# Splitting the activation quantization around four matmul blocks, with four PSUM banks, in an attention and FFN kernel on eight cores

## The reference, cut to what matters

```python
def act_quant(x):
    scale = 127.0 / jnp.clip(jnp.max(jnp.abs(x), axis=-1, keepdims=True), 1e-05)
    return jnp.clip(jnp.round(x * scale), -128, 127) / scale
...
h = bit_linear(x, w1)                       # 1024 -> 4096, ternary weights
h = depthwise_conv1d(h.transpose(0, 2, 1), conv_w, conv_b)   # 3 taps along the sequence
h = h.transpose(0, 2, 1)
h = jax.nn.silu(h)
return bit_linear(h, w2)                    # quantizes h per token, 4096 -> 1024
```

## Time and profile before

| | |
|---|---|
| Time, median of 2 executions | 5146.94 us (5120.43 and 5173.45) |
| Profiled execution | 5137.58 us |
| Span of its slowest core, core 3 | 5135.8 us |
| Spans of the eight cores | 5099.2 to 5135.8 us |
| DVE busy | 3280.5 us (64%) |
| PE matmul busy | 1809.6 us (35%) |
| ACT busy | 967.7 us (19%) |

### The profile page before, as it was taken

One profiled execution on the slowest core, in us unless ns is written; L12 is line 12 of the kernel. 1 busy time (PEld: TensorE's weight loads), 2 busy tenths in 40 slices (PEclk: granted clock), 3 DMA queues, 4 the chain that ended last, 5 costly groups with the idle time before them and its releaser, 6 DMA issues. The chain is left out here.

```text
span 5135.8 us, 35109 instructions; the slowest of 8 cores (5099.2 to 5135.8 us)
## 1 busy us (share of the span) xinstructions
PE 1809.6 (35%) x8500; PEld 904.4 (18%) x8500; DVE 3280.5 (64%) x4522; ACT 967.7 (19%) x1773; POOL 25.7 (0%) x52
## 2 busy tenths in 40 slices
PE   0046433227433203222222222222223322205999
PEld 0022111013111102111111111111111111102444
DVE  3213577712377767777787777777778777774343
ACT  2200122200022202222232222322223222200111
POOL 0000000000000000000000000000000000000000
PEclk9987666657766656666666666666666666657999
DMA  5521111131211122000000000000000000025443
GB/s 166 142 31 47 60 41 41 41 51 17 82 43 41 45 104 63 1 22 22 22 23 0 22 22 23 22 0 22 22 22 22 1 22 17 17 90 174 142 160 107
DMA packets 189264, 258.95 MB, mean 50 GB/s; under 512 B 63490, under 2 KB 131330, under 8 KB 187012
## 3 DMA queue, kind: packets, MB, share of 16 engines
q1 hardware_dynamic: 163716, 197.95, 12.6%
q10 hardware_dynamic: 18432, 41.97, 2.1%
q0 software_dynamic: 6912, 16.78, 2.1%
HBM read 188.47 MB, written 75.52 MB: 51 GB/s over the span
## 5 line engine op out<-in xcount | busy, mean ns | idle before, releaser
L849 PE MATMUL ps_a<-xqF,tw 128*128 128x258 bf16 (+1 forms) x2048 | 364.8, 337 | 1386.7 <-DVE ubuf L860 1174.9
L587 PE MATMUL ps_s<-kf,qf 128*128 128x512 bf16 x1024 | 296.8, 461 | 605.6 <-ACT disc L604 603.2
L849 PEld LDWEIGHTS ps_a<-xqF,tw 128*128 128x128 bf16 x2048 | 222.9, 116 | 1523.1 <-issue 1462.4
L873 ACT ACTIVATE vt<-ubuf,cbcol,cwcol 128x256 f32<-128x256 f32 x512 | 307.8, 601 | 969.6 <-DVE ubuf L860 966.9
L849 PE MATMUL ps_b<-xqF,tw 128*128 128x258 bf16 (+1 forms) x2048 | 340.4, 320 | 107.5 <-DVE ubuf L860 106.4
L797 DVE TENSOR_TENSOR accb<-accb,rbuf 128x2048 bf16<-128x2048 bf16 x256 | 313.5, 1225 | 19.4 <-issue 0.4
L743 DVE SCALAR_TENSOR_TENSOR vt<-ubuf,cwcol,vt 128x256 f32<-128x256 f32 x512 | 248.2, 485 | 82.5 <-issue 65.6
L758 ACT ACTIVATE ubuf<-vt 128x256 f32<-128x256 f32 x512 | 213.8, 418 | 337.5 <-DVE vt L750 337.5
L750 DVE SCALAR_TENSOR_TENSOR vt<-ubuf,cwcol,vt 128x256 f32<-128x256 f32 x512 | 248.2, 485 | 39.7 <-issue 1.7
L1011 PE MATMUL ps_c<-tw,hq 128*128 128x512 bf16 x512 | 195.3, 381 | 202.2 <-DMA hq<-hqs 202.2
L849 PEld LDWEIGHTS ps_b<-xqF,tw 128*128 128x128 bf16 x2048 | 216.8, 113 | 224.7 <-issue 170.4
(11 more groups left out here) (134 smaller groups left out, 2795.8 us busy)
## 6 DMA issues: line engine op xcount, KB each, us to landing
hqs<-hqst SPq DMA_DIRECT2D x16, 2048.0 KB, 8.8
wstage<-w1T SPq DMA_DIRECT2D x8, 2048.0 KB, 8.7
wstage<-w2T SPq DMA_DIRECT2D x32, 512.0 KB, 4.4
xres<-x_tm SPq DMA_DIRECT2D x32, 512.0 KB, 3.3
x1s<-x1t ACTq DMA_DIRECT2D x32, 512.0 KB, 9.1
qstage<-w1T SPq DMA_DIRECT2D x8, 2048.0 KB, 8.2
qstage<-w2T SPq DMA_DIRECT2D x32, 512.0 KB, 3.5
xres<-x1s SPq DMA_DIRECT2D x32, 512.0 KB, 8.0
```

Of the source, the lines that this page charges most:

```text
L587: t.matmul(ps_s[kb][:, 0:KBW], qf[:, dc * S + qcol: dc * S + qcol + 128], kf[:, dc * S + kb * KBW: dc * S + (kb + 1) * KBW], start=(dc == ...
L849: lo=lo, hi=hi, w0=w0, W=W: t.matmul(bank[:, 0:W], tw[:, dc * H + hc * 128: dc * H + hc * 128 + 128], xqF[:, (par * DC + dc) * WW + (lo - w0):
L873: p.op("scalar", lambda sc, hc=hc: sc.activation(out=vt1[:, (hc % 4) * T1W2:(hc % 4) * T1W2 + T1], in_=ubuf[:, hc * T1W2 + 1:hc * T1W2 + 1 ...
```

## The change

The quantization of a group is cut in two functions. `emit_quant_A` (L771, L782) stays in front of blocks 0, 8, 16 and 24. `emit_quant_B` (the wait for ACT, L787 to L800) comes in front of blocks 4, 12, 20 and 28; the wait for the store of the tile before the quantized one goes with it. For the last tile A and B follow each other directly, as before. PE uses four banks in turn (ps_a, ps_b, ps_s[0], ps_s[1]) and waits for the L860 of four blocks earlier. The convolution's tails come three blocks behind instead of two. No operation is added, removed or changed in size.

```diff
-        def emit_quant_group(i, g0):
+        qg_iqq = {}
+
+        def emit_quant_A(i, g0):
             ng = min(NQG, HC - g0)
             FD = ng * T1
             s28 = s2bc8[:, 0:FD]
-            if g0 == 0:
-                if i >= 1:
-                    p.wait("vector", stsems[(i - 1) % 2], st_cnt[i - 1])
...
             p.op("scalar", lambda sc, FD=FD: sc.activation(
                 out=iqq[:, 0:FD], in_=zscr[:, 0:FD], func=AF.Identity,
                 bias=c128[:, 0:1], scale=1.0), inc=ssm)
-            ev_iqq = ssm.n
-            p.wait("vector", ssm, ev_iqq)
+            qg_iqq[(i, g0 // NQG)] = ssm.n
+
+        def emit_quant_B(i, g0):
+            ng = min(NQG, HC - g0)
+            FD = ng * T1
+            if g0 == 0:
+                if i >= 1:
+                    p.wait("vector", stsems[(i - 1) % 2], st_cnt[i - 1])
+            p.wait("vector", ssm, qg_iqq[(i, g0 // NQG)])
...
             for hc in range(HC):
-                bank = ps_a if hc % 2 == 0 else ps_b
+                bank = (ps_a, ps_b, ps_s[0], ps_s[1])[hc % 4]
                 cpar = hc % 2
                 if i >= 1 and hc % NQG == 0:
-                    emit_quant_group(i - 1, hc)
-                    if hc == 0:
-                        pass
-                if hc >= 2:
-                    p.wait("tensor", vv, ev_u[(i, hc - 2)])
+                    emit_quant_A(i - 1, hc)
+                if i >= 1 and hc % NQG == NQG // 2:
+                    emit_quant_B(i - 1, hc - NQG // 2)
+                if hc >= 4:
+                    p.wait("tensor", vv, ev_u[(i, hc - 4)])
                 elif i >= 1:
-                    p.wait("tensor", vv, ev_u[(i - 1, HC - 2 + hc)])
+                    p.wait("tensor", vv, ev_u[(i - 1, HC - 4 + hc)])
...
-                if hc >= 2:
-                    emit_conv_tail(i, hc - 2)
-            emit_conv_tail(i, HC - 2)
-            emit_conv_tail(i, HC - 1)
+                if hc >= 3:
+                    emit_conv_tail(i, hc - 3)
+            for tl in range(HC - 3, HC):
+                emit_conv_tail(i, tl)
...
         for g0 in range(0, HC, NQG):
-            emit_quant_group(NT1 - 1, g0)
+            emit_quant_A(NT1 - 1, g0)
+            emit_quant_B(NT1 - 1, g0)
```

## The result

| | median | lowest to highest | executions |
|---|---|---|---|
| before | 5117.25 us | 5106.02 to 5173.45 | 10 |
| changed | 4997.59 us | 4992.21 to 5028.35 | 11 |

The ratio, which weighs all executions, is 0.9753 (95% interval 0.9718 to 0.9788): 2.5% faster. The medians are 119.7 us apart, 2.3%.

The account below looks back on a forecast made before the run. VectorE (DVE) was taken to bound the first FFN stage. Split -126.4, tile starts +18.3, tile 0's tail +0.4, old PE waits -0.6: -108.3 us from 5137.6 gives 5029 us, range 4998 to 5066.

Parts of the forecast that it names:

- the saving of the split: First FFN stage: 60 of 64 groups each swap a 2.267 us DVE stall for a 0.16 us seam, -126.4 us.
- The start of a tile: First four L860 of tiles after the first: 2.60 us waiting for PE against 1.38 before, +18.3 us in all.
- the race of tile 0: Tile 0's first four blocks, DVE waiting for PE's fills, fourth ready 6.56 us after PE's start; taken for later tiles.
- clock risen already in the third block: Lower bound at each tile's start: block 3 about 6.0 us after PE's start, 2.0 us wait, +9 us in all.
- The base: Whole kernel: the saving was subtracted from the profiled execution, 5137.6 us, not from the median of 5146.9.
- The range: Whole kernel: forecast bounds 5021 to 5038 widened by half of 53 us, given as 4998 to 5066 us.
- ACT behind the conversion: L873 queued behind the conversion ends 2.9 us after A, L743 needs it after 6.1: slack 3.2 us, no cost.
- The banks: Four PSUM banks instead of two: 0.6 us of old PE waits left to save, no bank late after the fourth block.
- (a): Rival, chance 0.12: PE stays at 1.2 GHz through every tile's start, +27.0 us there, 5038 us.
- (b): Rival, chance 0.05: nothing gained, stall reappears elsewhere or waits are not what DVE pays for; 5156 or 5138 us.
- (c): Rival, chance 0.03: the conversion beside L860 and the tail slows DVE; 5149 us if DVE stood still throughout.
- (d): Rival, chance 0.10: a group's two new seams cost 0.41 us each instead of 0.16, 30 us, so 5059 us.

Follow-up runs that it names:

- experiment 5: Changed kernel, with PE no longer waiting for the scaled f1bc at a tile's start: F1's stretch 2273.1 us (changed kernel 2295.0), median 4979.35 us.
- experiment 7: Changed kernel with PE's f1bc wait dropped and two PSUM banks instead of four: F1's stretch 2300.4 us (changed kernel 2295.0).
- experiment 8: Changed kernel with B two blocks behind A instead of four: F1's stretch 2280.6 us (changed kernel 2295.0).
- Experiment 9: Changed kernel with ACT doing each conversion twice, tails three behind: F1's stretch 2304.7 us (changed kernel 2295.0).
- experiment 4: Changed kernel with two PSUM banks again instead of four: F1's stretch 2294.5 us (changed kernel 2295.0).
- experiment 2: Kernel before with four PSUM banks and nothing else: F1's stretch 2392.5 us (before 2412.3), median 5123.82 us, ratio 0.9975.

## Why the prediction was right, and where it was wrong

**What bounds F1, and the saving of the split: right.** DVE sets the pace; 60 stalls went and left seams. L787's idle time was to fall from 145.1 to about 19 us, and fell to 20.5. The seam is 0.17 us behind one wait and 0.24 in the first group of a tile (2194.29 + 0.48 to 2195.01 in experiment 5's timeline), where the store's wait stands beside it; in tile 1, whose B has no store to wait for, it is 0.17. The prediction had taken this as +0.1 or -0.1 us and so as nothing, and it is nothing: L771/L770, where the wait had stood, lost 1.0 us.

**The start of a tile: right mechanism, mis-sized term.** The sum had +1.22 us a tile (+18.3 us in all) from the race of tile 0. L860/L866 lost only 6.1 us. That tile 1 met the forecast to 0.03 us is luck: tile 0 was taken for all 15, and PE's clock rises at different points of the first four blocks, so the waits are 1.15 to 2.63 us, mean 1.80, not 2.60. The cheaper bound, "clock risen already in the third block" (2.0 us), lies above this mean; in tile 2 the clock rose in the second block, which no bound covered, and the cost was 1.27. This is 12 us of the sum; dearer seams (1.8 us) and L743 (2.1 us, less 1.0 at L770) took 3 back. F1 saved 117.3 us where 108.3 were forecast. Experiments 5, 7 and 8 show that this place responds to PE's start, to the banks and to B's position.

**The base: wrong, and the larger error.** This is the step that failed. The sum was made against the profiled 5137.6 us. The median of ten executions of before is 5117.25. That is 20 us, and with the 9 us of F1 it makes 29 of the 31.7 us between 5029.3 and 4997.6. The first profile could have told: cores 2 and 3 had spans of 5131.5 and 5135.8 us and the other six 5099.2 to 5107.2, while all eight had the same F1. The slowest of eight cores was a late one, and the change doesn't touch what made it late. The slowest of the six would have given 5107.2 + 1.8 - 108.3 = 5001 us, the median of ten executions 5009. The range went wrong by the same step: 53 us between two executions were halved to both sides of the higher of the likely levels, though the fast end is where most executions lie (seven of ten at 5106 to 5120 us, the other three at 5155 to 5173). It is also not what its own recipe gives: the lower bound of 5021 less half of 53 us is 4994.5 and not 4998, the upper one 5064.5 and not 5066. With that sum done right the measured time would have lain inside, but near its end and for the same wrong base.

**ACT behind the conversion: right for the steady steps, too generous at a tile's start.** The slack of 3.2 us for L743 assumed three full steps of 1.79 us. At a tile's start four L866 follow each other without a tail: 5.15 us from A's end to the first L743 in tile 1, 3.8 in tile 2, against 2.9 for L879. Experiment 9 found the difference (0.67 us a tile with a doubled conversion), experiment 5 met it with the real one (0.49 us). That tails three behind are cover not needed was right; that they cost nothing was not: undone they save 4 us.

**The banks: right for the change, incomplete alone.** In the changed kernel they are worth nothing (experiment 4). The prediction left only 0.6 us for deeper banks, as it had counted the 1.38 us of each tile's third L860 into the tile's start; without the split the banks save these, 20 us in all (experiment 2).

**The rivals.** (a), a clock that stays low through each tile's start, falls: it wanted the fourth L866 7.14 us after PE's start, and over the 15 tiles it starts 5.1 to 6.6 us after it. The rule of the Trainium skill, "TensorE: Matmul & The Clock Gate", section "A second HAM failure mode: psum-queue depth-cycling", fits in that PE's fills alternate between 1.2 and 2.4 GHz in F1 (1.88 and 1.06 us), with two banks as with four (the granted clock of the stage is 0.64 and 0.63). It reaches the time only at a tile's start, as DVE sets the rest, and whether the cycling through banks is what lowers the clock is not shown here. (b) and the rule on the number of operations fall: the same DVE operations take 117 us less. (c) falls: the L743 that follow the conversion's start in the group shown still take 0.48 us, and the mean over all 512 is 485 ns as before. (d), dearer seams, falls: 0.17 and 0.24 us.

## What to carry to other kernels

Where the bounding engine waits for a short job of another, put its own independent work between request and use, and then look at what that work had been covering elsewhere: here A and B had covered PE's first blocks of a tile, and B two blocks behind A, or PE started earlier, gave the cover back. Before summing from a profile, compare the cores: a stage that the change doesn't touch and that is long only on some cores is no part of the base. Where executions scatter by more than the effect of an edit, the time between two instances of one repeated instruction measures the stage to 1 to 5 us (its spread over the eight cores in the kernels here).

## What the runs showed of the hardware that I had not expected

- A pair of cores runs part of the matmul stages at a lower granted clock (0.70 against 0.76 over 400 us, 0.94 against 1.00 over 430 us) and ends 25 to 35 us late; the pair and the stage change between executions (cores 2 and 3, 0 and 1, 4 and 5).
- After the same pause PE's clock rises now within the second block of eight matmuls, now only within the fourth: at tile 1 the third L866 waits 1.29 us and at tile 2 0.47 us, with PE's start at the same place in both.
- A second satisfied wait in front of a DVE instruction adds some 0.07 us to the 0.17 us of the first (L793 at the start of a tile: 0.17 us in tile 1, 0.23 to 0.25 in the tiles behind it but one).
